# Graph layer with residual and layer norm: the rearranged weight copy, the first node pairs, the resets and the tail

## The reference

```python
agg = jax.ops.segment_sum(x[src], dst, num_segments=n)
deg = jax.ops.segment_sum(jnp.ones((src.shape[0],), x.dtype), dst, num_segments=n)
mean = agg / jnp.maximum(deg, 1.0)[:, None]
h = mean @ W_l + b + x @ W_r
x = _layernorm(x + h * jax.nn.sigmoid(h), axis=-1)   # eps 1e-5
```

## Time and profile before

| | |
|---|---|
| median of 3 runs | 1550.5 us |
| the profiled execution, its own time | 1550.07 us |
| its span, first to last instruction | 1548.2 us |
| TensorE busy | 1501.8 us (97%) |
| VectorE, ScalarE, POOL busy | 1319.6, 1184.4, 1030.7 us |
| TensorE clock granted, mean | 0.989 of full speed |
| last matmul ends, about | 1533 us |

### The profile page before, as it was taken

One profiled execution on the slowest core, in us unless ns is written; L12 is line 12 of the kernel. 1 busy time (PEld: TensorE's weight loads), 2 busy tenths in 40 slices (PEclk: granted clock), 3 DMA queues, 4 the chain that ended last, 5 costly groups with the idle time before them and its releaser, 6 DMA issues.

```text
span 1548.2 us, 23957 instructions
## 1 busy us (share of the span) xinstructions
PE 1501.8 (97%) x7198; PEld 1244.3 (80%) x7198; DVE 1319.6 (85%) x2088; ACT 1184.4 (77%) x1609; POOL 1030.7 (67%) x1097
## 2 busy tenths in 40 slices
PE   7799999999999899999999999999999999999996
PEld 6687778888887787888888888888888888888884
DVE  7699999999998777888888888888888888888886
ACT  4354433333334698999999999999999999999996
POOL 6466556656662766667767777677677776776673
PEclk9899999999999999999999999999999999999998
DMA  5656589989997689999999999999999999999995
GB/s 193 173 178 192 166 247 266 266 259 272 267 267 232 176 258 265 277 283 276 276 271 268 280 298 270 281 287 273 268 281 281 289 280 279 280 277 275 290 270 184
DMA packets 298965, 397.68 MB, mean 257 GB/s; under 512 B 42652, under 2 KB 144822, under 8 KB 298837
## 3 DMA queue, kind: packets, MB, share of 16 engines
q1 hardware_dynamic: 250855, 321.43, 69.6%
q0 software_dynamic: 46944, 74.22, 18.0%
q10 hardware_dynamic: 1038, 0.50, 0.1%
HBM read 335.97 MB, written 139.67 MB: 307 GB/s over the span
## 4 chain that ended last, share of the span: by engine, by line
PE 80%; ACT 5%; DMA 5%; issue 4%; DVE 4%; POOL 1%; SPq 1%; POOLq 0%; ACTq 0%; DVEq 0%
PE pH L529 72%; PE pT L633 4%; PE pT L602 3%; DMA cor<-correction_rows,node_idx 2%; ACT O L804 2%; ACT cor L750 1%; PE pT L540 1%; ACT pH L816 1%; DMA X<-in_x 1%; POOL cor L441 1%; DMA light_x<-in_x 1%; DVE Z L904 1%; ACT Z L828 0%; DMA xs<-in_x 0%; DMA wr_raw<-in_L_gnn_W_r 0%
## 5 line engine op out<-in xcount | busy, mean ns | idle before, releaser
L441 POOL DMA_INDIRECT cor<-correction_rows,node_idx x347 | 395.7, 1140 | 224.8 <-ACT cor L750 150.1
L529 PE MATMUL pH<-ws_hi,x_hi 128*128 128x512 f32 x876 | 348.3, 398 | 7.6 <-ACT pH L816 4.5
L529 PE MATMUL pH<-ws_hi,x_lo 128*128 128x512 f32 x876 | 343.9, 393 | 0.0
L529 PE MATMUL pH<-ws_lo,x_hi 128*128 128x512 f32 x876 | 343.4, 392 | 0.0
L529 PE MATMUL pH<-wb_hi,x_hi 128*128 128x512 f32 x688 | 276.1, 401 | 0.0
L529 PE MATMUL pH<-wb_hi,x_lo 128*128 128x512 f32 x688 | 268.9, 391 | 0.0
L529 PE MATMUL pH<-wb_lo,x_hi 128*128 128x512 f32 x688 | 268.5, 390 | 0.0
L804 ACT ACTIVATE O<-Z,shift,rstd 128x512 f32<-128x512 f32 x347 | 261.9, 804 | 3.6 <-DVE shift L1127 3.6
L1117 DVE BATCH_NORM_STATS2 stats<-Z 128x6 f32<-128x512 f32 x347 | 219.3, 673 | 0.3 <-issue 0.3
L1109 DVE TENSOR_TENSOR Z<-Z,X 128x1024 f32<-128x1024 f32 x174 | 211.2, 1214 | 2.8 <-ACT Z L828 2.8
L725 ACT ACTIVATE s_hi<-sums 128x512 fp32r<-128x512 f32 x98 | 62.0, 633 | 192.3 <-DVE sums L1028 192.3
(11 more groups left out here) (148 smaller groups left out, 2765.1 us busy)
## 6 DMA issues: line engine op xcount, KB each, us to landing
X<-in_x SPq DMA_DIRECT2D x173, 512.0 KB, 4.6
out<-O SPq DMA_DIRECT2D x173, 512.0 KB, 5.3
xs<-in_x SPq DMA_DIRECT2D x344, 128.0 KB
correction_rows<-c_out SPq DMA_DIRECT2D x98, 256.0 KB, 4.2
light_x<-in_x SPq DMA_DIRECT2D x58, 256.0 KB, 2.8
light_h<-early_product SPq DMA_DIRECT2D x44, 256.0 KB
out<-light_o SPq DMA_DIRECT2D x44, 256.0 KB, 4.3
join_row<-joined SPq DMA_DIRECT2D x98, 64.0 KB, 4.1
```

What stands on the lines that cost most here:

```text
L441: g.indirect_dma_start(out=out_, out_offset=None, in_=table, in_offset=bass.IndirectOffsetOnAxis(ap=idx, axis=0), bounds_check=bound, oob_ ...
L529: last = mm(ps, a[:, k], w[:, k], start=(n == 0 and not onto), stop=(n == len(terms) - 1), skip_group_check=onto)
```

## The change

- SP no longer loads rearranged weights. After `merged` it copies `ws_hi` and `ws_lo` to `wb_hi` and `wb_lo` inside SBUF, 32 transfers of 32 partitions x 2 KB (64 KB each), four behind each of the early steps 19 to 26. POOL's four additions and four subtractions and ScalarE's four roundings go.
- Pairs 0 to 3 (`ADDED = 4`) get their correction from VectorE after the product; seeding begins with pair 4. Up to pair 4 ScalarE rounds the next pair ahead of SiLU.
- ScalarE resets `light_cor` in edge tile ET-9 and one `cor` buffer in each of ET-8, ET-7 and ET-6. The product of early tile 42 is emptied ahead of `round_sums(0)`. POOL gathers pairs 0 and 1 ahead of the light tile.
- The light steps of the last two pairs are doubled (`lights`), and the tail is reordered: the last light tile is finished ahead of the last pair.

```diff
+        def lights(light, t):
+            first = t if t < NP - 2 else 2 * t - NP + 2
+            for k in range(first, first + (1 if t < NP - 2 else 2)):
                 light(k // 4, k % 4)
+        def last_lights(light):
+            for k in range(NP + 2, NP + 6):
+                light(k // 4, k % 4)
...
             peeled(0, 8, move_early)
-            sp.wait_ge(wl_split, K)
-            for w, tile in ((w_l, wb_raw), (w_r, xs)):
-                for i in range(4):
-                    sp.dma_start(tile[32 * i:32 * i + 32], w[i * P:(i + 1) * P].rearrange("(k a) n -> a k n", a=32)
-                                 ).then_inc(wb_in, 16)
-            peeled(8, EARLY - 8, move_early)
+            peeled(8, COPIED, move_early)
+            sp.wait_ge(ws_split, K)
+            sp.wait_ge(wl_split, K)
+            sp.wait_ge(merged, 2)
+            for n in range(2 * K):
+                single(COPIED + n, move_early)
+                copied, from_ = (wb_hi, ws_hi) if n < K else (wb_lo, ws_lo)
+                i = n % K
+                for k in range(K):
+                    sp.dma_start(copied[32 * i:32 * i + 32, k].bitcast(f32), from_[32 * k:32 * k + 32, i].bitcast(f32)).then_inc(wb_in, 16)
+            peeled(COPIED + 2 * K, EARLY - 8, move_early)
...
-            pool.wait_ge(wb_in, 128)
-            for k in range(K):
-                g.tensor_tensor(wb_raw[:, k], wb_raw[:, k], xs[:, k], ALU.add).then_inc(wb_summed, 1)
-                single(14 + k, split_early)
...
-            gather_light(0)
             single(0, gather_cor)
             single(1, gather_cor)
+            gather_light(0)
             single(2, gather_cor)
...
+                elif t < ADDED:
+                    pe.wait_ge(z_made, t - 1)
                 else:
-                    pe.wait_ge(seeded, t - 1)
+                    pe.wait_ge(seeded, t - ADDED + 1)
...
-                if fixed(t) and t == ET - 5:
+                if t == ET - 9:
                     act.wait_ge(idx_ready, 1)
                     reset_light(0)
-                    single(0, reset_cor)
-                    single(1, reset_cor)
-                    single(2, reset_cor)
+                if ET - 8 <= t < ET - 5:
+                    single(t - (ET - 8), reset_cor)
...
-                shifted(t, q, u, -1, NP, silu)
-                shifted(t, q, u, 1, NP, round_x)
-                if t >= 1:
+                if t <= ADDED:
+                    shifted(t, q, u, 1, NP, round_x)
+                    shifted(t, q, u, -1, NP, silu)
+                else:
+                    shifted(t, q, u, -1, NP, silu)
+                    shifted(t, q, u, 1, NP, round_x)
+                if t + 1 >= ADDED:
                     shifted(t, q, u, 1, NP, seed)
                 shifted(t, q, u, 3, NP, reset_cor)
-                light(q, u)
+                lights(light, t)
...
-                if t == 1 or t == 2:
+                if 1 <= t <= ADDED:
                     single(t - 1, add_cor)
...
             single(NP - 2, moments)
+            single(NP - 2, make_shift)
             single(NP - 1, residual)
             single(NP - 1, moments)
-            single(NP - 2, make_shift)
-            light_tail(light, NP, 4 * EARLY)
+            last_lights(light)
             single(NP - 1, make_shift)
-            light_tail(light, 4 * EARLY, 4 * EARLY + 4)
```

More of the change, by code:

```diff
@@ L34, in gnn_layer @@
     assert (NTILES - EARLY) % 2 == 1 and ET % 2 == 0 and NP % 2 == 0 and COLS <= 512
-    assert EARLY - 1 == NP // 4
+    assert 4 * EARLY == NP + 2
     LATE = 28
+    ADDED = 4
+    COPIED = 4 * MERGE_ROUND + 3
     assert BITS - ROW_BITS <= COLS.bit_length()
@@ L224, in peeled @@
                 step(t, t // 4, t % 4)
-        def light_tail(light, first, end):
-            for k in range(first, end):
+        def lights(light, t):
[4 more added lines that the diff above has]
+            for k in range(NP + 2, NP + 6):
                 light(k // 4, k % 4)
@@ L377, in move @@
                 shifted(t, q, u, -3, NP, store_out)
-                light(q, u)
+                lights(light, t)
             peeled(0, NP, move)
-            light_tail(light, NP, 4 * EARLY)
-            for t in range(NP - 3, NP):
-                single(t, store_out)
-            light_tail(light, 4 * EARLY, 4 * EARLY + 4)
+            single(NP - 3, store_out)
+            single(NP - 2, store_out)
+            last_lights(light)
+            single(NP - 1, store_out)
             sp.wait_ge(light_stored, 16 * EARLY)
@@ L421, in _ @@
                 single(4 + k, split_early)
-            peeled(8, 14, split_early)
-            pool.wait_ge(wb_in, 128)
-            for k in range(K):
-                g.tensor_tensor(wb_raw[:, k], wb_raw[:, k], xs[:, k], ALU.add).then_inc(wb_summed, 1)
-                single(14 + k, split_early)
[L427 to L433, removed]
+            peeled(8, 4 * FIND_ROUND, split_early)
             pool.wait_ge(dst_ready, 1)
@@ L486, in light_make_rstd, with light_first, light_last @@
                 g.tensor_tensor(l_rstd[:], l_var_eps[:], minus_half[:, 0:1], ALU.pow).then_inc(light_rstd, 1)
+            def light_first(q, u):
+                if u == 0:
+                    light_at(q - 1, light_make_rstd)
+            def light_last(q, u):
+                if u == 2:
+                    light_at(q + 1, gather_light)
             def make_rstd(t, q, u):
@@ L711, in _ @@
             peeled(1, 8, early_tile)
[L712 to L717, removed]
-            peeled(4 * MERGE_ROUND + 2 + K, EARLY - 4, early_tile)
+            peeled(8, EARLY - 4, early_tile)
             def round_sums(t, q, u):
@@ L745, in reset_cor @@
             def reset_cor(t, q, u):
-                if t == 4 or t == 5:
-                    act.wait_ge(z_made, t - 3)
-                wait(act, seeded, t - 5)
+                if t - 4 < ADDED:
+                    wait(act, z_made, t - 3)
+                else:
+                    act.wait_ge(seeded, t - 4 - ADDED + 1)
                 a_(cor[u][:], bias_rows[:].rearrange("p (a n) -> p a n", a=1).to_broadcast([P, 2, D]), ACT.Copy
@@ L810, in seed @@
                 b, used = ring(q, u, 4)
-                wait(act, silu_made, t - 1)
+                if t - 2 < ADDED:
+                    act.wait_ge(z_made, t - 1)
+                else:
+                    act.wait_ge(silu_made, t - 1)
                 if nt == 2:
```

22 lines of the change are left out of this document (10 added, 12 removed).

## The result

| | before | changed |
|---|---|---|
| median, same chip | 1550.64 us (6 runs, 1549.07 to 1552.09) | 1542.89 us (6 runs, 1538.16 to 1544.13) |
| ratio | | 0.9946, 95% interval 0.9931 to 0.996 |
| the profiled execution, its span | 1550.07, 1548.2 us | 1544.13, 1542.3 us |

The kernel became 7.8 us faster. Forecast were 16.1 us, with 1528 to 1542 us as the range, so the sign was right and the size about twice too large.

What follows compares the result with a forecast made beforehand. TensorE's own pace, 5.9 us a pair, was taken as the bound, so gains lie only in its waits, slow clock and tail. 10.7 - 3.5 + 1.1 + 5.6 + 2.2 = 16.1 us gave 1534.4 us, range 1528 to 1542.

Steps and rivals of the forecast that it cites:

- Part 1, the stall at tile 10: Early tiles 9 to 11: without the eight weight loads the transposes lie two paces apart, 10.7 us gained.
- VectorE's edge list: Early stage: put at no cost; as a rival (6%) it becomes the bound and costs 3 us, 1537.4 us.
- Part 1, the copies: Early tiles 22 to 27: loads two steps ahead stand behind four copies on SP, 3.5 us lost.
- My upper bound, 7.9 us: Loss at tiles 22 to 27 if each copy holds the transfer queue 0.9 us; the lower bound was 2.7 us.
- One sign that I had named for being wrong: Early stage: ending less than 6 us sooner would show the forecast wrong.
- Part 2: Edge stage: resets spread one per tile no longer hold the next edge tile's `hi`, 1.1 us gained.
- Part 3: First pairs: seed wait and slow matmuls of 7.0 us go, less 1.4 us of new lateness, 5.6 us gained.
- I take 0.7 us there and as much again at pairs 4 and 5, 1.4 us: First pairs: VectorE's extra additions make it late at pair 3, then pairs 4 and 5; bounds 0 and 7.0 us.
- So pair 2 isn't held, by a margin of 0.5 us: First pairs: `lo` of pair 2 ready by 509.9 us, TensorE free for it at 510.4 us.
- only moves: First pairs, rival (13%): the wait moves to late `lo`, loads to `X` or pair 4's gather; 5.6 us gain gone, 1540.0 us.
- Part 4: Steady pairs: unchanged; a wait like pair 16's load to `X`, 5.0 us in all, expected again, no gain counted.
- Part 5, the tail: End of kernel: light tile finished ahead of the last pair, ending at 1540.9 instead of 1543.1, 2.2 us gained.

Runs made afterwards that it cites:

- part1_only: Kernel before with its weight loads replaced by the copies at tiles 19 to 26, nothing else: 1546.84 us against 1550.65 us (0.9968).
- resets_back: Changed kernel with ScalarE's five resets all at edge tile ET-5, as before: 1542.84 us, one run.
- late_shift: Changed kernel with copies seven steps later and VectorE's shift of pairs 0 to 3 one step later: 1530.22 us against 1547.12 us before (0.9891).
- again_before: Kernel before, unchanged, run again on another chip: 1546.26 us, one run, beside a further run of it at 1548.09 us.
- act_copies: Changed kernel with the same 32 copies at the same steps issued from ScalarE's queue instead of SP's: 1533.99 us (0.9926 against before).
- rep_after: Changed kernel once more, unchanged, with its own profile: 1538.97 us against 1546.79 us for the kernel before (0.9947).

## Why the prediction was wrong, point by point

- **Part 1, the stall at tile 10: right.** 10.7 us forecast, 10.65 measured. VectorE's edge list did not become the bound: VectorE still stands for 15.35 us in the list, now for POOL (row below), and the stretch from tile 28 to the first edge product is 63.50 us after 63.63.

```profile
123.14 0.21 DVE L981 TENSOR_SCALAR dst_idx<-O 128x98 int32<-128x98 int32 x1 [15.35 <-POOL O L436]
```

- **Part 1, the copies: right mechanism, size too small.** The failed term is 3.5 us for "each of these six loads now stands behind four copies on SP"; it measured 5.9 to 6.3 us against the profile of before (7.1 in part1_only), and 6.5 to 6.8 us against seven undisturbed paces. The sum had 7.3 us a turn of two tiles. The turns from tile 20 to 26 take 8.45, 8.00 and 8.52 us, 5.8 us over six paces. In the first, the load goes 2.55 us behind the first copy and not 1.88: I took the issue of a copy, 0.47 us, from loads of whole tiles. The rest is 3.30 us from the load's issue to the transpose, where I had 2.8. In the later turns the issue of a load to `X` stands in the queue besides. My upper bound, 7.9 us, held the value; the choice near the lower end, by the bytes, was the mistake, since the bytes were not what cost. A reading in that bound was off as well: the nine transfers landed between 41.35 and 49.92 us, 1.07 us apart and not 0.9. One sign that I had named for being wrong came true: the early stage ends 4.0 us sooner (first edge product at 173.79 us after 177.83), less than 6.
- **Part 2: right within what the profiles tell.** 1.1 us forecast; 0.9 to 2.3 us by resets_back, 0.1 to 1.5 us by the profile of before, and the wait of 1.08 us returns with the old resets.
- **Part 3: 5.6 us forecast, 2.5 to 3.2 measured** against the profile that the forecast was made from; the other two with the old order have 50.57 and 50.43 us, up to 1.1 us less than it. Seed and slow matmuls went, as said: the clock granted from 510 to 520 us is 1.00 and was 0.66. The step that failed is "I take 0.7 us there and as much again at pairs 4 and 5, 1.4 us". I counted VectorE's work and left out that it stands for POOL's `rstd` in between, behind the gathers. The table gives 3.8 to 4.5 us above the floor for pairs 0 to 8 where I allowed 1.4; late_shift gave 2.0 of it back. A second step failed before it: "So pair 2 isn't held, by a margin of 0.5 us". The second gather of pair 0 did come 1.2 us sooner, counted from the transposes of pair 0, but the addition began 4.10 us behind that gather's start and not 3.15, the `lo` of pair 2 ended at 512.60 us, and TensorE began pair 2 at 512.69 after 0.56 us idle. The rival "only moves" (13%) came half true. The gather and the addition:

```profile
506.13 1.00 POOL L441 DMA_INDIRECT cor<-correction_rows,node_idx  x1 [0.30 <-issue]
...
510.23 1.23 DVE L1110 TENSOR_TENSOR Z<-pH,cor 128x1024 f32<-128x1024 f32 x1 [5.28 <-DMA cor<-correction_rows,node_idx]
```

- **Part 4: the wait at pair 16 is chance.** I kept 5.0 us of it. It is absent in again_before (70.68 us for pairs 8 to 20, the floor), so it belonged to one execution. In the changed kernel pairs 8 to 20 take 73.3 to 76.3 us: a seed is late by 1.78 us at pair 10 instead, behind a gather that stands with 8.12 us in the chain of waits. No clear gain or loss.

```profile
564.87 0.47 PE L535 MATMUL pH<-ws_hi,x_hi 128*128 128x512 f32 x1 [1.78 <-ACT pH L821]
```

- **Part 5, the tail: right.** 2.2 us forecast, 2.1 to 2.35 measured in the three profiles of the changed kernel. Over all fourteen with the new tail it is 0.8 (act_copies) to 2.4 us; the cause in act_copies stays open. Last is the 80-row normalisation:

```profile
1536.36 0.81 ACT L806 ACTIVATE O<-Z,shift,rstd 80x512 f32<-80x512 f32 x1 [0.26 <-DVE shift L1135]
```

- **The rest.** With the measured terms, 10.65 - 6.2 + 1.1 + 2.8 + 2.2 is 10.6 us, and the medians gave 7.8 twice (the first runs, and rep_after). The missing 2.8 us are not shown to be the stop: rep_after's profile has none, and its span is still only 9.0 us below that of before. It holds two losses without a term in the forecast: 0.5 us between tiles 11 and 21 (36.12 us after 35.60, and 36.1 to 36.2 in all but one profile with the copied weights), and 2.6 us in the steady pairs (904.90 after 902.33), which is what executions differ by: 901.8 to 904.9 us with no change to them. Where the median lost them stays open, and the range left little room for such differences.

## What to carry to other kernels

Before small transfers are put in front of loads on a queue, count the queue's issue time for their own shape, and ask how many steps ahead the loads behind them are: the same 32 copies cost 6 us where loads are two steps ahead and some 0.6 us seven tiles later. Where a wait is removed by giving an engine more work, list that engine's waits for others as well as its work; an operation that waits for a slow partner may be moved one step later, as the shift was here, with 2.0 us gained in that stretch and no new wait of that size. A wait that stands once in one profile should be looked for in a second one before it is kept in, or left out of, a sum; and before a cause in the kernel is sought for it, the profiles with and without it should be compared for missing records.

## What was not expected of the hardware

- The issue of a 64 KB copy between 32-partition pieces of SBUF took 0.59 us on SP's queue in the median, that of a 256 KB load of a tile 0.43. While copies were under way a load's issue took longer, whichever queue issued the copies: 0.58 us behind them on SP's queue, 0.56 to 0.67 us with the copies on ScalarE's. What lengthens it is not shown.
- A stop of 3.24 to 3.32 us of VectorE near 356 us in six profiles and of 0.80 us near 350 us in two, behind a late signal of TensorE, in just the eight of 17 profiles whose landings were not all recorded.
